# The stacks of the first two images, loaded one image at a time from two queues, at the seam between the two stages of a vision-transformer kernel

## The chip, the cores and the metric

The kernel runs on one core of a Trainium2 chip. The time is the device time of one execution in microseconds (us). The core has TensorE (PE in the profile, its weight loads PEld), VectorE (DVE), ScalarE (ACT), GpSimd (POOL) and the sync engine (SP). SP, ACT and POOL issue DMA transfers; the profile calls SP's and ACT's issuing SPq and ACTq. Each engine takes its instructions in order, so a wait or a transfer to be issued holds up all that is behind it on that engine. Sixteen DMA engines carry the transfers.

## The reference, cut to what matters

```python
h = concat([images] + four_shifted_crops).patches() @ W + b     # 128 images, 196 tokens, D = 192
h = concatenate([cls_tok, h], axis=1)                            # 197 tokens
xn = layernorm(h)
q, k, v = xn @ Wq.T, xn @ Wk.T, xn @ Wv.T                        # 6 heads of 32
scores = q @ k.T / sqrt(32) + lam * (q . anchor)                 # softmax over the keys
h = h + softmax(scores) @ v @ Wo.T
h = h + int8_quantised(layernorm(h) / 0.02) @ weight_t * 0.0002 + bias
```

## The kernel before

There are two stages. `build_tokens` makes the tokens of all 128 images, one row of patches at a time (14 rows), and writes the tokens and their normalised form to the DRAM scratches `h_dram` and `xn_dram`. `build_attention` then goes through the images with `images(eng, step)`: each engine runs `step(i)` for i = -5 to 131, and in one step different images are at different points of a pipeline. In step i, image i+5 is turned, image i+1 is scored, image i is exponentiated, image i-1 is attended, and older images go on through output projection and the last layer. Every engine has its own written order, with semaphores between them. Images 0 to 11 and the last 12 steps are written out; the middle is a loop over six images.

The work around the change, for one pair of images, is:

- `load_xn` (SP, L748 and L749) brings an image's normalised tokens to `xn_in`. PE turns them (`turn`, L822) into a PSUM bank, `MISC[2]`. ACT copies the rounded value to `x_hi` (L1052), DVE the rest to `x_lo` (L1219). PE waits for these before it turns the next image into the same bank (L1006).
- `project_block` (PE, L841) makes a block of q and k columns for both images of a pair at once: block 0 (q of heads 0 to 3), block 1 (q of heads 4 and 5, k of heads 0 and 1), block 2 (k of heads 2 to 5). ACT writes `qk_hi` (L1065) and DVE `qk_lo` (L1150). The partitions there are sorted by dimension and head. Before block 0 is written, ACT and DVE wait until the transfers of the pair before have landed (L1064, L1149), since these still read the buffer.
- `stack` (SP, L741) copies them within the on-chip memory to `q_st` and `k_st`, where each head has 32 partitions for each of three rows: q is stacked as high, high, low and k as high, low, high. That is 12 transfers for a pair: six of 128 packets of 1,584 bytes (198 values of one head for both images) and six of 64. All count on `stacked[pair]`, and `score(n, 0)` waits for 192 of it (12 times 16). Blocks 0 and 1 are made and stacked in an odd step, block 2 in the next, even one.
- `score` (PE, L873) multiplies q by k for one head, and DVE takes the maximum of each row (`maxima`, L1135). After six heads DVE splits the maxima (L1229, L1231), PE turns them (L1042), ACT copies them to `max_rows` (L1052), and SP puts them into two further partitions of `q_st` (L798). `score_t` (PE, L887) uses them, and `exps` (ACT, L1058) follows.

For pair 0, blocks 0 and 1 are made in step -3 and block 2 in step -2. Image 0 is scored in step -1, where also pair 2 (images 2 and 3) has its blocks 0 and 1. Image 1 is scored in step 0, image 2 in step 1, where image 0 is attended (L897).

Three things are done once between the stages. POOL fills the constant rows `key_rows` (L1315, L1317) and then works out the norm factors of the last tokens (L140 to L148). From the factors DVE makes the last `xn_t` (L1257), SP stores it (L804), and SP's first `load_xn` waits for it. ACT copies `key_rows` into all of `k_st` (L1125). POOL fills the maxima's rows of `q_st` (L1330).

Of the kernel before, what the change touches and what calls it, by code (L numbers as in the profile page):

```python
# [5 lines left out]
F32 = mybir.dt.float32  # L6
# [620 lines left out]
def build_attention(nc, s):  # L627
# [65 lines left out]
    stacked = [sem(f"stacked{i}") for i in range(NP)]  # L693
    max_landed = [sem(f"max_landed{i}") for i in range(MOD)]
# [41 lines left out]

    with nc.Block() as block:
        @block.sync
        def _(sp):
# [11 lines left out]
            def step(i):  # L751
# [6 lines left out]
                if p.within(B) and i.r % 2:  # L758
                    q_first, q_last, k_first = (0, 4), (4, H), (0, SPLIT)
                    q_rows, k_rows = slice(0, SPLIT * HD), slice(SPLIT * HD, BLOCK)  # L760
# [32 lines left out]
                if a.within(B):  # L793

                    if a.fixed and a.n == 0:
                        sp.wait_ge(no_score_made, 1)
                    sp.wait_ge(mrow_done, a.count(1, 1))
                    sp.dma_start(q_st[ST:ST + 2, a.pair, :, a.two, :].bitcast(F32), max_rows[:, a.two, :].bitcast(F32))\  # L798
                        .then_inc(max_landed[a.slot], 16)

# [16 lines left out]
        def _(pe):  # L817
# [48 lines left out]
            def score(n, h):  # L866

                if h == 0:
                    pe.wait_ge(stacked[n.pair], n.landed(192))
# [59 lines left out]
            def step(i):  # L929
# [70 lines left out]
                if has_f:  # L1000
# [4 lines left out]
                    elif f.plus(-1).within(B):  # L1005
                        pe.wait_ge(xhi_done, f.count(1, 0))  # L1006
                        pe.wait_ge(xlo_done, f.count(1, 0))
                    turn(MISC[2], xn_in, f.slot % NX, (DA, 2 * DB)).then_inc(xt_done, 1)
# [41 lines left out]
        def _(act):  # L1050
# [9 lines left out]
            def high(p, block, bank):  # L1060
                act.wait_ge(qk_done, p.pair_count(3, block + 1))
                if block == 0 and p.reuses(2):
                    before = p.plus(-2)
                    act.wait_ge(stacked[before.pair], before.landed(192))  # L1064
                nc.scalar.activation(qk_hi[:, block, :], bank[:, 0:2 * TP], ACT.Copy).then_inc(qkhi_done, 1)  # L1065

            def step(i):
# [10 lines left out]
                elif has_p:  # L1078
                    high(p, 2, MISC[2])
                    if has_c:  # L1080
                        exps(c, 5)
                if has_c:
# [7 lines left out]
                if has_f:  # L1090
# [3 lines left out]
                    copy(x_hi[:, f.pair, f.two, :, :], wide(MISC[2], DA), xhi_done)  # L1094
# [10 lines left out]
                if has_a:  # L1105
# [4 lines left out]
                    copy(max_rows[:, a.two, :], o_bank[0:2 * H, 1, 0:TP], mrow_done)  # L1110
                if has_g:
# [18 lines left out]
        def _(dve):  # L1130
# [14 lines left out]
            def low(p, block, bank):  # L1145
                dve.wait_ge(qkhi_done, p.pair_count(3, block + 1))
                if block == 0 and p.reuses(2):
                    before = p.plus(-2)
                    dve.wait_ge(stacked[before.pair], before.landed(192))  # L1149
                nc.vector.tensor_tensor(qk_lo[:, block, :], bank[:, 0:2 * TP], qk_hi[:, block, :].bitcast(F32),  # L1150
                                        ALU.subtract).then_inc(qklo_done, 1)

            def step(i):
# [60 lines left out]
                if has_f:  # L1214
# [3 lines left out]
                    for ic, rows_in in enumerate((DA, DB)):  # L1218
                        last = nc.vector.tensor_tensor(x_lo[0:rows_in, f.pair, f.two, ic, :],  # L1219
                                                       wide(MISC[2], rows_in)[:, ic, :],  # L1220
# [93 lines left out]

# [58 lines left out]
```

## Time and profile before

| | |
|---|---|
| time, median of 3 runs | 1737.6 us (1737.4 to 1737.8) |
| the profiled execution's own time | 1740.1 us |
| its span, first to last instruction | 1738.4 us |
| PE busy | 1649.2 us (95%) |
| DVE busy | 1471.8 us (85%) |
| POOL busy | 924.5 us (53%) |
| ACT busy | 759.3 us (44%) |
| last token work of the first stage to image 0's attention | 415 to 476 us |

Times of rows are us from the span's start. The clock of PE is given as a share of 2.4 GHz: 1.00 or 0.50 (1.2 GHz). A row of the timeline has its start, its duration, the engine, the line of the kernel, what it writes and reads, and in brackets how long the engine was idle before it and what ended that. The profiled execution's own time is 1.7 us over its span, and 2.5 us over the median of the runs.

### The profile page before, as it was taken

The numbers are of one execution on the slowest core, as the hardware profiler recorded it, in microseconds if no ns is written. First come the engines' busy times: TensorE is split into PE (matmuls) and PEld (weight loads), VectorE is DVE, ScalarE is ACT, GpSimd is POOL, SyncE is SP. The second block draws the span as 40 slices with busy tenths as digits, with TensorE's granted clock in tenths as the row PEclk, the third lists the DMA queues.
The fourth block names the chain that finished last, engine by engine and source line by source line (L and its number), as shares of the span: only waits on it lengthen the run. The fifth ranks groups of instructions, "written<-read, shape, count | busy, mean of one in ns | idle before, by whom it ended". The sixth has DMA issues, their size and how long they took to land.

```text
span 1738.4 us, 53263 instructions
## 1 busy us (share of the span) xinstructions
PE 1649.2 (95%) x16368; PEld 1500.8 (86%) x16368; DVE 1471.8 (85%) x3906; ACT 759.3 (44%) x1751; POOL 924.5 (53%) x1911
## 2 busy tenths in 40 slices
PE   4999999996599999999999999999999999999996
PEld 4999999995588888888888888888888888888884
DVE  7888888895388888888888888888888888888885
ACT  2000000001255555655556565555656555565653
POOL 3353443536056555555655565565556555555555
PEclk9999999997699999999999999999999999999998
DMA  9899989973787778877788777878787777877761
GB/s 300 269 306 298 322 283 307 325 250 131 114 141 154 143 137 149 147 150 144 139 147 150 146 142 146 147 148 150 134 150 150 146 143 142 147 148 148 139 122 33
DMA packets 214814, 303.66 MB, mean 175 GB/s; under 512 B 47584, under 2 KB 203667, under 8 KB 204644
## 3 DMA queue, kind: packets, MB, share of 16 engines
q1 hardware_dynamic: 204718, 228.10, 65.4%
q10 hardware_dynamic: 6054, 38.54, 7.5%
q0 software_dynamic: 3984, 36.28, 5.4%
q8 instruction: 32, 0.52, 0.1%
q14 instruction: 26, 0.21, 0.0%
HBM read 126.54 MB, written 58.29 MB: 106 GB/s over the span
## 4 chain that ended last, share of the span: by engine, by line
PE 46%; DVE 8%; POOL 8%; issue 7%; DMA 3%; SPq 2%; ACT 0%; POOLq 0%; DVEq 0%; ACTq 0%
PE bank L841 8%; PE o_bank L897 7%; PE bank L887 6%; PE bank L873 6%; PE bank L850 4%; PE bank L862 4%; PE o_bank L822 2%; POOL ln L163 2%; DMA k_st<-qk_lo 2%; DVE neg_max L1135 2%; POOL qx L1309 2%; PE o_bank L925 2%; PE o_bank L916 2%; PE bank L822 2%; PE bank L972 2%
## 5 line engine op out<-in xcount | busy, mean ns | idle before, releaser
L1058 ACT ACTIVATE probs<-bank 99x396 f32<-99x396 f32 x768 | 381.8, 497 | 218.8 <-PE bank L887 218.5
L1276 POOL TENSOR_TENSOR key_sum<-probs 99x396 f32<-99x396 f32 x256 | 227.5, 889 | 438.5 <-ACT probs L1058 289.6
L1135 DVE TENSOR_REDUCE neg_max<-bank 99x2 f32<-99x394 f32 x768 | 419.7, 561 | 25.7 <-PE bank L873 21.8
L340 PE MATMUL bank<-e_t,xt 128*128 128x192 f32 x2352 | 388.0, 329 | 25.4 <-DVE xt L448 21.7
L340 PEld LDWEIGHTS bank<-e_t,xt 128*128 128x128 f32 x2352 | 386.4, 192 | 26.6 <-DVE xt L448 26.4
L873 PE MATMUL bank<-k_st,q_st 96*99 96x198 f32 x1536 | 275.0, 274 | 17.8 <-DMA k_st<-qk_lo 11.6
L887 PE MATMUL bank<-q_st,k_st 99*99 99x198 f32 x1536 | 280.9, 264 | 6.9 <-DMA q_st<-max_rows 4.1
L448 DVE STREAM_TRANSPOSE xt<-x_t 128x256 f32<-128x256 f32 x588 | 215.0, 416 | 45.0 <-PE bank L340 43.5
L887 PEld LDWEIGHTS bank<-q_st,k_st 99*99 99x99 f32 x1536 | 207.9, 166 | 51.7 <-issue 44.3
L873 PEld LDWEIGHTS bank<-k_st,q_st 96*99 96x99 f32 x1536 | 192.7, 167 | 34.4 <-issue 13.5
L897 PE MATMUL o_bank<-probs,vals 99*32 99x198 f32 (+1 forms) x3072 | 197.1, 335 | 0.0
L1052 ACT ACTIVATE o_t<-o_bank 128x396 f32<-128x396 f32 x128 | 64.1, 501 | 232.6 <-PE o_bank L916 232.6
L897 PEld LDWEIGHTS o_bank<-probs,vals 99*32 99x32 f32 (+1 forms) x3072 | 112.9, 109 | 46.3 <-ACT probs L1058 0.2
L916 PE MATMUL o_bank<-key_sum,pick 99*32 99x198 f32 x1536 | 150.8, 330 | 0.0
L1309 POOL TENSOR_SCALAR qx<-h,ln 99x192 f32<-99x192 f32 x256 | 127.0, 503 | 40.1 <-POOL ln L163 40.1
L1288 POOL TENSOR_TENSOR hb<-h,ffn_bias 99x384 f32<-99x384 f32 x128 | 129.2, 1009 | 2.7 <-DVE h L1197 2.7
L349 ACT ACTIVATE ffn_w_bf<-ffn_raw 96x384 bf16<-96x384 int8 x1 | 0.5, 522 | 294.4 <-issue 294.4
L163 POOL TENSOR_TENSOR ln<-ln,minus_half 99x2 f32<-99x2 f32 x128 | 114.1, 892 | 23.1 <-POOL ln L162 23.1
L1150 DVE TENSOR_TENSOR qk_lo<-bank,qk_hi 128x396 fp32r<-128x396 f32 x192 | 108.3, 564 | 18.8 <-ACT qk_hi L1065 17.7
L1065 ACT ACTIVATE qk_hi<-bank 128x396 fp32r<-128x396 f32 x192 | 96.1, 501 | 60.4 <-PE bank L841 54.0
L862 PE MATMUL bank<-wo_hi,a_mix 128*99 128x192 f32 x512 | 120.3, 253 | 0.0
L862 PE MATMUL bank<-wo_lo,a_mix 128*99 128x192 f32 x512 | 120.2, 253 | 0.0
(134 smaller groups left out, 3589.4 us busy)
## 6 DMA issues: line engine op xcount, KB each, us to landing
x_t<-in_x_dram SPq DMA_DIRECT2D x26, 1344.0 KB, 20.5
x_t<-in_x_dram ACTq DMA_DIRECT2D x26, 1344.0 KB, 22.0
q_st<-qk_hi SPq DMA_DIRECT2D x128, 198.0 KB, 4.3
k_st<-qk_hi SPq DMA_DIRECT2D x128, 198.0 KB, 4.5
xn_in<-xn_scratch SPq DMA_DIRECT2D x128, 148.5 KB
h_in<-h_scratch SPq DMA_DIRECT2D x128, 148.5 KB
h_scratch<-h_t POOLq DMA_DIRECT2D x13, 1344.0 KB, 17.7
xn_scratch<-xn_t POOLq DMA_DIRECT2D x13, 1344.0 KB, 8.0
```

Source lines behind the costliest of these rows:

```text
L163: link(nc.gpsimd.tensor_tensor(v[6], v[5], half, ALU.pow))
L340: last = pe.matmul(token_bank(p)[:, 0:D], xt[:, p, c // 3, c % 3, :], e_t[:, row_kind(t), col, c // 3, c % 3, :], start=c == 0, stop=c == 5)
L448: last = nc.vector.transpose(xt[:, p, :, c, :].rearrange("p m (g b) -> p g m b", b=32), pix[:, c])
L862: last = pe.matmul(bank[0:TC, c * D:(c + 1) * D], inputs, weights, start=i == 0, stop=i == len(pairs) - 1)
L873: last = pe.matmul(S_BANK[h % 2][0:TC, c * TP:(c + 1) * TP], q_st[0:ST, n.pair, h, n.two, c * TC:(c + 1) * TC], k_st[0:ST, n.pair, h, n.tw ...
L887: last = pe.matmul(T_BANK[0:TC, c * TP:(c + 1) * TP], k_st[:, n.pair, h, n.two, c * TC:(c + 1) * TC], q_st[:, n.pair, h, n.two, :], start= ...
L897: pe.matmul(o_bank[at % 4 * HD:(at % 4 + 1) * HD, 0, col:col + TP], vals[0:kk, n.two, kc, h, :], probs[0:kk, n.two, h, kc, :], start=kc == ...
L916: last = pe.matmul(o_bank[to:to + HD, 0, TP:2 * TP], pick[:, j, :], key_sum[:, n.two, HEAD_AT[side * HG + j], :], start=j == 0, stop=j == ...
L1058: nc.scalar.activation(probs[:, n.two, h, :, :], wide(T_BANK, TC), ACT.Exp).then_inc(exp_done, 1)
L1135: nc.vector.tensor_reduce(out=neg_max[:, n.two, :, h], in_=wide(S_BANK[h % 2], TC)[:, :, 0:NTOK], axis=AX_X, op=ALU.max, negate=True).then ...
L1276: nc.gpsimd.tensor_tensor(key_sum[:, b.two, heads, :], probs[:, b.two, heads, 0, :], probs[:, b.two, heads, 1, :], ALU.add).then_inc(pool_ ...
L1309: nc.gpsimd.tensor_scalar(qx[:, e.two, cc, :], h1[:, e.two, cc, :], v[7][:, cc:cc + 1], v[6][:, cc:cc + 1], ALU.add, ALU.mult).then_inc(ln ...
```

## The change

For images 0 and 1 alone, the transfers of the stack take one image each (24 transfers of 792-byte packets in place of 12 of 1,584). SP issues those of q and ACT those of k, image 0's first. Image 0 counts on a semaphore of its own. The maxima's rows of images 0 and 1 are stored by ACT and no longer by SP. Image 1 is turned into `MISC[0]` in place of `MISC[2]`, without the wait for image 0's copies. POOL works out the last norm factors before it fills `key_rows`. The code for all later images is as it was.

```diff
+    first_stacked = sem("first_stacked")
...
+    def leads(n):
+        return n.fixed and 0 <= n.n < 2
+    def stack_one(eng, image, dst, row, heads, src):
+        eng.dma_start(dst[row * HD:(row + 1) * HD, 0, heads[0]:heads[1], image, :].bitcast(F32),
+                      src[:, image * TP:(image + 1) * TP].bitcast(F32))\
+            .then_inc(stacked[0] if image else first_stacked, 16)
+    def store_max_rows(eng, a):
+        if a.fixed and a.n == 0:
+            eng.wait_ge(no_score_made, 1)
+        eng.wait_ge(mrow_done, a.count(1, 1))
+        eng.dma_start(q_st[ST:ST + 2, a.pair, :, a.two, :].bitcast(F32), max_rows[:, a.two, :].bitcast(F32))\
+            .then_inc(max_landed[a.slot], 16)
+    def turned_into(f):
+        return MISC[0] if f.fixed and f.n == 1 else MISC[2]
...
+                if leads(p) and i.r % 2:
+                    sp.wait_ge(qkhi_done, p.pair_count(3, 1))
+                    stack_one(sp, 0, q_st, 0, q_first, qk_hi[:, 0, :])
+                    stack_one(sp, 0, q_st, 1, q_first, qk_hi[:, 0, :])
+                    sp.wait_ge(qklo_done, p.pair_count(3, 1))
+                    stack_one(sp, 0, q_st, 2, q_first, qk_lo[:, 0, :])
+                    sp.wait_ge(qkhi_done, p.pair_count(3, 2))
+                    stack_one(sp, 0, q_st, 0, q_last, qk_hi[q_rows, 1, :])
+                    stack_one(sp, 0, q_st, 1, q_last, qk_hi[q_rows, 1, :])
+                    sp.wait_ge(qklo_done, p.pair_count(3, 2))
+                    stack_one(sp, 0, q_st, 2, q_last, qk_lo[q_rows, 1, :])
+                elif leads(p):
+                    stack_one(sp, 1, q_st, 0, q_first, qk_hi[:, 0, :])
+                    stack_one(sp, 1, q_st, 1, q_first, qk_hi[:, 0, :])
+                    stack_one(sp, 1, q_st, 2, q_first, qk_lo[:, 0, :])
+                    stack_one(sp, 1, q_st, 0, q_last, qk_hi[q_rows, 1, :])
+                    stack_one(sp, 1, q_st, 1, q_last, qk_hi[q_rows, 1, :])
+                    stack_one(sp, 1, q_st, 2, q_last, qk_lo[q_rows, 1, :])
+                elif p.within(B) and i.r % 2:
...
-                if a.within(B):
-                    if a.fixed and a.n == 0:
-                        sp.wait_ge(no_score_made, 1)
-                    sp.wait_ge(mrow_done, a.count(1, 1))
-                    sp.dma_start(q_st[ST:ST + 2, a.pair, :, a.two, :].bitcast(F32), max_rows[:, a.two, :].bitcast(F32))\
-                        .then_inc(max_landed[a.slot], 16)
+                if a.within(B) and not leads(a):
+                    store_max_rows(sp, a)
...
-                if h == 0:
+                if h == 0 and n.fixed and n.n == 0:
+                    pe.wait_ge(first_stacked, 192)
+                elif h == 0:
                     pe.wait_ge(stacked[n.pair], n.landed(192))
...
-                    elif f.plus(-1).within(B):
+                    elif f.plus(-1).within(B) and not leads(f):
                         pe.wait_ge(xhi_done, f.count(1, 0))
                         pe.wait_ge(xlo_done, f.count(1, 0))
-                    turn(MISC[2], xn_in, f.slot % NX, (DA, 2 * DB)).then_inc(xt_done, 1)
+                    turn(turned_into(f), xn_in, f.slot % NX, (DA, 2 * DB)).then_inc(xt_done, 1)
...
                     act.wait_ge(stacked[before.pair], before.landed(192))
+                    if leads(before):
+                        act.wait_ge(first_stacked, 192)
...
+                k_rows, k_first, k_last = slice(SPLIT * HD, BLOCK), (0, SPLIT), (SPLIT, H)
+                if leads(p) and odd:
+                    act.wait_ge(qkhi_done, p.pair_count(3, 2))
+                    stack_one(act, 0, k_st, 0, k_first, qk_hi[k_rows, 1, :])
+                    stack_one(act, 0, k_st, 2, k_first, qk_hi[k_rows, 1, :])
+                    act.wait_ge(qklo_done, p.pair_count(3, 2))
+                    stack_one(act, 0, k_st, 1, k_first, qk_lo[k_rows, 1, :])
+                elif leads(p):
+                    act.wait_ge(qkhi_done, p.pair_count(3, 3))
+                    stack_one(act, 0, k_st, 0, k_last, qk_hi[:, 2, :])
+                    stack_one(act, 0, k_st, 2, k_last, qk_hi[:, 2, :])
+                    act.wait_ge(qklo_done, p.pair_count(3, 3))
+                    stack_one(act, 0, k_st, 1, k_last, qk_lo[:, 2, :])
+                    stack_one(act, 1, k_st, 0, k_first, qk_hi[k_rows, 1, :])
+                    stack_one(act, 1, k_st, 2, k_first, qk_hi[k_rows, 1, :])
+                    stack_one(act, 1, k_st, 1, k_first, qk_lo[k_rows, 1, :])
+                    stack_one(act, 1, k_st, 0, k_last, qk_hi[:, 2, :])
+                    stack_one(act, 1, k_st, 2, k_last, qk_hi[:, 2, :])
+                    stack_one(act, 1, k_st, 1, k_last, qk_lo[:, 2, :])
...
-                    copy(x_hi[:, f.pair, f.two, :, :], wide(MISC[2], DA), xhi_done)
+                    copy(x_hi[:, f.pair, f.two, :, :], wide(turned_into(f), DA), xhi_done)
...
                     copy(max_rows[:, a.two, :], o_bank[0:2 * H, 1, 0:TP], mrow_done)
+                    if leads(a):
+                        store_max_rows(act, a)
...
+            made = [0]
+            def link_last(ins):
+                made[0] += 1
+                ins.then_inc(last_row_ln, 1)
+                pool.wait_ge(last_row_ln, made[0])
+            norm_factors(nc, link_last, stats[:, LAST, EARLY:G, :], [ln[:, LAST, i, EARLY:G] for i in range(8)],
+                         minus_half[:, 0:G - EARLY])
 
             pool.memset(key_rows[ST:ST + 3, :], 1.0).then_inc(rows_made, 1)
             pool.wait_ge(rows_made, 1)
...
-            made = [0]
-            def link_last(ins):
-                made[0] += 1
-                ins.then_inc(last_row_ln, 1)
-                pool.wait_ge(last_row_ln, made[0])
-            norm_factors(nc, link_last, stats[:, LAST, EARLY:G, :], [ln[:, LAST, i, EARLY:G] for i in range(8)],
-                         minus_half[:, 0:G - EARLY])
             pool.wait_ge(last_row_xn, G - EARLY)
```

DVE's wait at L1149 and its read of the bank at L1220 are changed as ACT's are.

## Rows read from the trace of the kernel before

**Rows 1.** The chain of work that ended last, 380 to 495 us: start, us, what.
```profile
415.41 0.27 POOL key_rows L1315
...
416.18 0.22 POOL ln L140
...
421.71 2.78 DMA xn_scratch<-xn_t
...
434.37 0.73 SPq L741
...
443.23 7.99 DMA k_st<-qk_lo
...
461.36 3.27 DMA q_st<-max_rows
...
491.38 0.61 PE bank L873 x4
...
494.22 0.96 PE o_bank L897 x18
```

**Rows 2.** Timeline of the loads and projections, 416 to 442 us.
```profile
416.13 6.14 ACT L1052 ACTIVATE k_st<-key_rows 3x7128 fp32r<-3x7128 f32 x1 [84.43 <-POOL key_rows L1317]
...
425.74 0.40 SPq L749 DMA_DIRECT2D xn_in<-xn_scratch  x1
...
427.35 0.89 PE L822 MATMUL bank<-ident,xn_in 99*128 99x99 f32 x4 [14.04 <-DMA xn_in<-xn_scratch]
...
429.58 0.89 PE L822 MATMUL bank<-ident,xn_in 99*128 99x99 f32 x4 [1.34 <-DVE x_lo L1219]
...
435.49 0.50 ACT L1065 ACTIVATE qk_hi<-bank 128x396 fp32r<-128x396 f32 x1 [1.15 <-PE bank L841]
...
436.15 0.50 ACT L1052 ACTIVATE x_hi<-bank 128x396 fp32r<-128x396 f32 x1 [0.16 <-PE bank L822]
...
439.48 0.50 ACT L1065 ACTIVATE qk_hi<-bank 128x396 fp32r<-128x396 f32 x1 [2.83 <-PE bank L841]
```

**Rows 3.** Issue times of lines 261 and 741 (ns: least/median/most); landing of the latter.
```profile
L261 SPq DMA_DIRECT2D x_t<-in_x_dram x16: 433/482/2285, 3.7 to 15.4; - x16
L261 ACTq DMA_DIRECT2D x_t<-in_x_dram x16: 351/500/804, 6.6 to 14.8; - x16
...
L741 SPq DMA_DIRECT2D k_st<-qk_hi x256: 567/598/1966, 438.1 to 1681.0; - x128
...
DMA to landing us min/median/max: 2.8/4.6/8.0
```

**Rows 4.** DMA queue in 438 to 440, 443 to 445, 425 to 430: packets, MB, share.
```profile
q1 hardware_dynamic: 186, 0.26, 106.4%
...
q1 hardware_dynamic: 359, 0.30, 115.1%
...
q1 hardware_dynamic: 1429, 0.74, 57.0%
```

**Rows 5.** Timeline of images 0 to 2, 451 to 476 us.
```profile
453.98 0.50 ACT L1065 ACTIVATE qk_hi<-bank 128x396 fp32r<-128x396 f32 x1 [11.82 <-PE bank L841]
...
459.22 0.33 ACT L1052 ACTIVATE max_rows<-o_bank 12x198 fp32r<-12x198 f32 x1 [2.82 <-PE o_bank L1042]
...
464.37 0.61 SPq L741 DMA_DIRECT2D k_st<-qk_lo  x1
...
471.23 0.96 PE L873 MATMUL bank<-k_st,q_st 96*99 96x198 f32 x4
...
475.67 1.04 PE L897 MATMUL o_bank<-probs,vals 99*32 99x198 f32 x18
```

**Rows 6.** Busy time of PE, PEld, DVE, ACT, POOL by stretch, clock, DMA share, GB/s.
```profile
457.90:461.30 3.40, 2.19 (x18) 1.82 (x16) 2.12 (x7) 1.20 (x3) 0.00 (x0) 1.00 1.08 143
461.30:464.70 3.40, 0.00 (x0) 0.00 (x0) 0.79 (x2) 0.00 (x0) 0.00 (x0) 1.00 0.97 175
464.70:468.10 3.40, 3.08 (x16) 2.80 (x16) 1.01 (x2) 1.61 (x4) 0.85 (x1) 0.50 1.09 134
```

More of the change, by code:

```diff
@@ L757, in step @@
                     load_xn(ahead)
-                if p.within(B) and i.r % 2:
-                    q_first, q_last, k_first = (0, 4), (4, H), (0, SPLIT)
-                    q_rows, k_rows = slice(0, SPLIT * HD), slice(SPLIT * HD, BLOCK)
+                q_first, q_last, k_first = (0, 4), (4, H), (0, SPLIT)
+                q_rows, k_rows = slice(0, SPLIT * HD), slice(SPLIT * HD, BLOCK)
+                if leads(p) and i.r % 2:
[17 more added lines that the diff above has]
+                elif p.within(B) and i.r % 2:
                     sp.wait_ge(qkhi_done, p.pair_count(3, 1))
@@ L1149, in low @@
                     dve.wait_ge(stacked[before.pair], before.landed(192))
+                    if leads(before):
+                        dve.wait_ge(first_stacked, 192)
                 nc.vector.tensor_tensor(qk_lo[:, block, :], bank[:, 0:2 * TP], qk_hi[:, block, :].bitcast(F32),
@@ L1219, in step @@
                         last = nc.vector.tensor_tensor(x_lo[0:rows_in, f.pair, f.two, ic, :],
-                                                       wide(MISC[2], rows_in)[:, ic, :],
+                                                       wide(turned_into(f), rows_in)[:, ic, :],
                                                        x_hi[0:rows_in, f.pair, f.two, ic, :].bitcast(F32), ALU.subtract)
@@ L1310, in step @@
                                             v[6][:, cc:cc + 1], ALU.add, ALU.mult).then_inc(ln2_step, 1)
-            pool.memset(key_rows[ST:ST + 3, :], 1.0).then_inc(rows_made, 1)
-            pool.wait_ge(rows_made, 1)
-            pool.affine_select(out=key_rows[ST:ST + 3, 0:NTOK], in_=key_rows[ST:ST + 3, 0:NTOK], compare_op=ALU.is_ge,
-                               fill=0.0, base=1, pattern=[[0, NTOK]], channel_multiplier=-1).then_inc(rows_made, 1)
-            pool.wait_ge(rows_made, 2)
             made = [0]
@@ L1328, in _ @@
                          minus_half[:, 0:G - EARLY])
+            pool.memset(key_rows[ST:ST + 3, :], 1.0).then_inc(rows_made, 1)
+            pool.wait_ge(rows_made, 1)
+            pool.affine_select(out=key_rows[ST:ST + 3, 0:NTOK], in_=key_rows[ST:ST + 3, 0:NTOK], compare_op=ALU.is_ge,
+                               fill=0.0, base=1, pattern=[[0, NTOK]], channel_multiplier=-1).then_inc(rows_made, 1)
+            pool.wait_ge(rows_made, 2)
             pool.wait_ge(last_row_xn, G - EARLY)
```

## The prediction

> **What bounds the kernel now.** I read the chain of work that ended last first, around the change of stage. It goes through each thing that the diff touches: POOL's constant rows, the norm factors, the store and load of the last tokens, two turns, the projections, a series of issues of SP, and then the last transfer of the first stack, which is 7.99 us under way. PE starts on image 0's scores at 451.22. Ten microseconds later the chain waits again, for the maxima's rows, issued at 461.36 and landed at 464.63 [rows 1]. The timeline gives the starts between these [rows 2, 5], the stretches the clock [rows 6], the lines' own view what an issue costs [rows 3], and the DMA view what a packet costs [rows 4]. All of this is start-up, and it happens once. From image 2 on the code is the same, and what comes later waits for PE, DVE and POOL through semaphores and for no fixed moment, so what the start-up gains or loses should stay to the end. The whole question is by how much image 0's attention, now at 475.67 [rows 5], moves.
>
> **Step 1, the constant rows.** The norm factors start at 415.41 in place of 416.18 [rows 1]: 0.77 us less on the path. What moves behind them is ACT's copy of 6.14 us, which began at 416.13 [rows 2]. The nine factor instructions end near 419.1, POOL's two instructions 0.7 later, so the copy runs from 419.8 to 426.0. ACT is wanted for image 0 when the first turn ends, 427.35 + 0.89 - 0.77 = 427.5 [rows 2]. It is covered with 1.5 us to spare. If POOL must wait behind DVE's work on the last tokens until 420.9, 0.4 us comes back.
>
> **Step 2, the other bank.** Image 1's turn starts at 429.58, 1.34 after the first ends, having waited for the copies of image 0 [rows 2]. In another bank that wait goes: at most 1.34. But its tokens are issued up to 425.74 + 0.40, one load behind image 0's. I take 1.0 (bounds 0 and 1.34). The first stack transfer goes out at 434.37 - 0.77 - 1.0 = 432.6 [rows 1].
>
> **Step 3, what ACT's transfers hold up.** ACT's issues cost what SP's do (0.50 to 0.48 where both load), and a stack's costs 0.60 [rows 3]. ACT sends three right after `qk_hi` of block 1, now at 435.49 + 0.50 - 1.77 = 434.2. Behind them in ACT's order is `x_hi` of image 2, on which block 2 waits by way of `x_lo`. It would start at 436.15 - 1.77 = 434.4 [rows 2], and starts after 3 x 0.64 at 436.15. So block 2 gains nothing: its `qk_hi` is written at 439.5 as before. The last transfer of image 0's k goes out at 439.5 + 0.5 + 2 x 0.64 = 441.3, against 443.23, since it is the third and not the twelfth in its queue. Six more for image 1 end at 445.8. Only then comes `x_hi` of image 3, done in `x_lo` by 447.0, which pair 2's block 0 needs.
>
> **Step 4, image 0's stack lands.** 441.3 plus 2.8 to 7.99 [rows 1, 3]. The longest was with 11 others ahead. Here image 1's q is in the way. I take 4.7: 446.0 (444.1 to 449.3), five microseconds earlier than before.
>
> **Step 5, image 1's stack is the next wait.** PE can score heads 0 and 1 of image 0 and make pair 2's block 0, which takes 2.7 (451.26 to 453.98) and so ends at 448.8 or, by `x_lo`, 449. But the copies out of it wait for both semaphores, that is for image 1's transfers too, because `qk_hi` and `qk_lo` are read until then. On DVE `qk_lo` stands ahead of the maxima of heads 2 to 5, so image 0 waits as well. When does image 1 land? Before, 1152 packets of 1,584 bytes and the loads between them took from 434.37 to 451.22, 16.85 us, with the DMA engines full. Now there are 2304 packets of 792. A packet cost 2 us x 16 x 1.064 / 186 = 183 ns at a mean of 1.4 KB, and 2 x 16 x 1.151 / 359 = 103 ns at 0.84 KB; with nothing behind them loads' packets of 0.52 KB cost 5 x 16 x 0.57 / 1429 = 32 ns [rows 4]. So cost goes nearly by bytes: half the size is 0.55 of the price. 1152 x 183 ns / 16 is 13.2 us of packets, and the new ones take 1.1 times as long, 1.3 more. 432.6 + 16.85 + 1.3 = 450.8; I take 451.0. The bounds are 449.5 (nothing added) and, with 183 ns for every packet however short, 432.6 + 16.85 + 13.2 = 462.6.
>
> **Step 6, the maxima's rows.** From pair 2's first `qk_hi` to `max_rows` is 459.22 - 453.98 = 5.24, then 0.33 for it [rows 5]. ACT issues at once, where SP had nine stack transfers to send first, until 461.36. The transfer takes 3.27 in that crowd [rows 1], perhaps 2.3 without one; I take 3.0. `score_t` of image 0 starts at 451.0 + 0.1 + 5.24 + 0.33 + 3.0 + 0.1 = 459.8, against 464.8: 5.0 us gained.
>
> **Step 7, pair 2's stack and the clock.** SP sends k's last part of pair 2 after its own nine. Before, at 464.37, with the maxima's issue (0.7) between; now at 464.37 - 2.9 - 0.7 = 460.8, as it starts at 451.6 and not 454.5. It lands some 5.8 later, 466.6, and image 2's first scores, before at 471.23, wait for it: 4.6 gained. Before, TensorE stood from 460.7 to 464.8 (0.00 busy in 461.3 to 464.7), and the granted clock went from 1.00 to 0.50 (2.4 to 1.2 GHz); with 2.19 of 3.40 busy it had stayed [rows 6]. Now the holes are about 2 and 3 us, no stretch is empty, and I take the clock to stay. From those scores to the attention it took 475.67 - 471.23 = 4.44 at the low clock [rows 5], but 494.22 - 491.38 = 2.84 a pair later at the high one [rows 1]: 1.6 more. **Sum: 4.6 + 1.6 = 6.2 us.** The profiled execution would take 1740.1 - 6.2 = 1733.9. It lies 2.5 over the median of the runs, so the median becomes 1731.4.
>
> The Trainium skill ("DMA: Bandwidth & Descriptors", Rules for kernel authors) says that spreading transfers over SP, ACT and GpSimd gives no bandwidth, since all run on the same 16 DMA engines, and saves issue time alone. By it step 5 would have no faster end at all. No row of this trace has two full queues side by side.
>
> **The rivals.** What 0.2% is here, 3.5 us, is about what a measurement can tell from no change.
>
> - Likeliest, 54%: the above. Its own range is step 5 at 449.5 to 452.5 and step 7 with 1 us either way: 4.3 to 8, so 1729.6 to 1733.3.
> - Faster still, 10%: the two queues write different partitions at once and image 1 lands by 448, so that PE alone sets block 0's copies at 448.8. The gain is 5.2 + 2.2 (step 6) + 1.0 of clock: 1729.2. For it: at a share of 1.08 the engines moved 143 GB/s and at 0.97 175 GB/s [rows 6], so it is not the number of engines alone that sets the rate. Against: the share is full already with one queue, 1.06 to 1.15 [rows 4]. The Trainium skill ("SBUF — State Buffer", Door 1: The DMA port swizzle) puts partitions 0 to 63 on one half of the ports and 64 to 127 on the other, which is what could let q and k rows pass each other.
> - Partly lost, 16%: a short packet costs 0.65 of a long one (image 1 lands at 453.5) and TensorE's clock falls as before. 464.8 - 462.3 = 2.5 gained, none from the clock: 1735.1.
> - It doesn't do what it says, 8%: image 0 starts earlier, but pair 2's block 0, its stack and the maxima's rows all end as late as ever for ACT's nine issues and the wait for image 1, and only steps 1 and 2 remain: 1.8 gained, 1735.8.
> - Slower, 12%: cost goes by packets. The most is 462.6 in step 5, 8.6 after 453.98; less 2.1 for step 6 it is 6.5 lost, 1744.1. It turns to a loss where image 1 lands after 456, that is where a 792-byte packet costs over 0.75 of one of 1,584 (137 ns). The 103 ns speak against it, but those packets came from DRAM, and no row has on-chip packets of 792 bytes in a crowd.
>
> **How the numbers follow.** The likeliest gives 1731.4. Down to 1728.5 takes in nearly all of the faster case; up to 1738.5 takes in both cases of little gain and the near half of the slower one. Faster by over 0.2% is the first two, 0.64; within it, the next two, 0.24; slower 0.12.
>
> **What would show it.** Steps 1 and 2: the last tokens' store issued 0.8 earlier, a second turn right behind the first, the first stack issue near 432.6. Step 3: ACT's `x_hi` of image 2 still at 436. Steps 4 and 5: image 0's scores near 446, and pair 2's first `qk_hi` waiting for a transfer until 451; the number to look at. Step 6: `score_t` near 459.8. Step 7: clock 1.00 from 455 on, attention at 469.5. The prediction is wrong if packets of half the size cost well over half, if ACT's issues take far over 0.6 with full queues, or if the clock falls again.

## The result, and the profile after

The changed kernel takes 1735.98 us (median of 15 runs, 1732.44 to 1738.53), the kernel before, run beside it, 1738.18 (15 runs, 1737.0 to 1743.06). The ratio is 0.9983, with an interval of 0.9976 to 0.9991: some 2.9 us or 0.17% faster (the medians lie 2.2 us apart). The forecast was a gain of 6.2 us. The time lies inside the range (1728.5 to 1738.5), above the likeliest case's own 1729.6 to 1733.3, and by the 0.2% bound it counts as no change, to which I had given 0.24. That it lies inside is owed to the width of the range, which took in the cases of little gain; the gain is under half of what the sum gave.

The chain of work of the changed kernel that ended last, from 420 to 490 us (start, us, what), against [rows 1]:

```profile
421.98 2.77 DMA xn_scratch<-xn_t
...
426.01 2.92 DMA xn_in<-xn_scratch
428.98 0.94 PE bank L855 x4
...
431.24 3.65 PE bank L874 x10
...
435.45 0.69 ACTq L744
...
441.34 0.58 ACTq L744
...
446.53 1.84 DMA k_st<-qk_lo
448.51 2.00 PE bank L874 x5
450.53 0.51 ACT qk_hi L1102
451.06 0.57 SPq L762
...
460.24 7.48 DMA k_st<-qk_lo
467.76 0.98 PE bank L908 x4
...
489.10 0.62 PE bank L908 x4
```

The wait for image 0's stack is gone from it. In its place stand ScalarE's own issues, three at 435.45 and nine from 441.34. Then comes pair 2's stack, whose last transfer is 7.48 us under way. The start of image 4's scores, the last row, moved from 491.38 [rows 1] to 489.10, the 2.3 us of the whole.

The timeline of the same kernel shows the starts that answer to [rows 2, 5]:

```profile
428.98 0.92 PE L855 MATMUL bank<-ident,xn_in 99*128 99x99 f32 x4 [0.41 <-DMA xn_in<-xn_scratch]
...
437.48 0.50 ACT L1087 ACTIVATE x_hi<-bank 128x396 fp32r<-128x396 f32 x1 [2.06 <-issue]
...
445.97 0.98 PE L908 MATMUL bank<-k_st,q_st 96*99 96x198 f32 x4 [3.02 <-DMA k_st<-qk_lo]
...
447.20 0.50 ACT L1087 ACTIVATE x_hi<-bank 128x396 fp32r<-128x396 f32 x1 [5.89 <-issue]
...
456.36 0.33 ACT L1087 ACTIVATE max_rows<-o_bank 12x198 fp32r<-12x198 f32 x1 [2.35 <-PE o_bank L1077]
...
460.72 0.62 PE L922 MATMUL bank<-q_st,k_st 99*99 99x198 f32 x2 [2.92 <-DMA q_st<-max_rows]
...
467.76 0.98 PE L908 MATMUL bank<-k_st,q_st 96*99 96x198 f32 x4 [0.28 <-DMA k_st<-qk_lo]
...
472.74 1.61 PE L932 MATMUL o_bank<-probs,vals 99*32 99x198 f32 x18
```

Where stage one ends differs from one profiled execution to the next by up to 4 us, in code that no kernel here changes. So I count every start from SP's store of the last tokens, `h_scratch<-h_t`, which was issued at 415.41 before and 416.29 after. By it, in us (the forecast is the prediction's moment less 415.41):

| start of | before | forecast | after | gained |
|---|---|---|---|---|
| first stack transfer | 18.96 | 17.2 | 17.51 | 1.45 |
| image 0's first scores | 35.85 | 30.6 | 29.68 | 6.17 |
| pair 2's first `qk_hi` | 38.57 | 35.7 | 34.24 | 4.33 |
| `max_rows` of image 0 | 43.81 | 40.9 | 40.07 | 3.74 |
| transposed scores of image 0 | 49.36 | 44.4 | 44.43 | 4.93 |
| image 2's first scores | 55.82 | 51.2 | 51.47 | 4.35 |
| attention of image 0 | 60.26 | 54.1 | 56.45 | 3.81 |

Of 3.81 us at attention, 0.58 goes behind it and 0.88 is stage one's difference in this pair of executions. 2.35 us are left between the spans, 1738.4 and 1736.1. The 0.58 is gone by the end of attention itself: from its first matmul to the copy of its result (`o_t`) it took 475.67 to 477.60, 1.93 us at a granted clock of 1.00, before, and 472.74 to 475.24, 2.50 us at a mean clock of 0.76, after.

### The profile page after: what moved, and what is told of

Read it like the earlier page. It is cut to its first block, busy times and chain, and to the rows that moved or that the text cites. A ratio compares the mean times of both kernels' runs of the same rounds, so it can differ in the third digit from the quotient of the medians.

```text
span 1736.1 us, 53274 instructions
## 1 busy us (share of the span) xinstructions
PE 1655.0 (95%) x16368; PEld 1504.7 (87%) x16368; DVE 1471.9 (85%) x3906; ACT 759.4 (44%) x1751; POOL 925.9 (53%) x1911
## 4 chain that ended last, share of the span: by engine, by line
PE 50%; DVE 8%; POOL 7%; issue 7%; DMA 2%; SPq 1%; ACT 0%; ACTq 0%; POOLq 0%; DVEq 0%
PE bank L874 9%; PE o_bank L932 8%; PE bank L922 6%; PE bank L908 6%; PE bank L895 5%; PE bank L883 5%; PE o_bank L855 3%; PE o_bank L951 2%; PE bank L855 2%; PE o_bank L960 2%; POOL ln L163 2%; DVE neg_max L1193 2%; PE bank L1007 2%; DMA k_st<-qk_lo 2%; POOL qx L1369 2%
## 6 DMA issues: line engine op xcount, KB each, us to landing
h_scratch<-h_t POOLq DMA_DIRECT2D x13, 1344.0 KB, 17.2
```

## The experiments

Each ratio is against the kernel before on the same chip, where not said otherwise.

### What makes image 1 land early: short packets, not the second queue

**e5** keeps both queues and sends whole pairs, packets of 1,584 bytes in 12 transfers.

```diff
-eng.dma_start(dst[..., image, :], src[:, image * TP:(image + 1) * TP])
+if image == 0:
+    eng.dma_start(dst[row * HD:(row + 1) * HD, 0, heads[0]:heads[1], :, :], src)
```

All twelve count on `stacked[0]` again, so image 0's scores wait for both images.

> The changed kernel, but each of the 12 transfers of pair 0 takes both images again (packets of 1,584 bytes), q from SP and k from ACT as in the change. Theory A (the short packets are what made the transfers land in 2.6 to 3.1 us): here they take 4 to 8 us as in the kernel before, a packet costs 150 to 200 ns, and image 0's scores start at 449 to 451. Rival B (two queues are what made it fast): landing stays near 3 us, a packet near 70 ns, and the scores start at 446 or earlier; the time is that of the changed kernel or less, since ACT has six issues and not twelve.

Measured: 1739.25 us, ratio 1.0 (0.999 to 1.0009). The changed kernel has 0.9983 (0.9976 to 0.9991) from other runs, and the two intervals just touch. Image 0's scores come at 34.73 from the store and pair 2's first `qk_hi` at 37.45. The DMA view of its 431 to 448 us (queue, packets, MB, share of 16 engines), landings below:

```profile
q1 hardware_dynamic: 1490, 1.31, 52.9%
q10 hardware_dynamic: 672, 0.91, 38.6%
...
q_st<-qk_hi SPq DMA_DIRECT2D x2, 198.0 KB, 4.3
k_st<-qk_hi ACTq DMA_DIRECT2D x2, 198.0 KB, 6.9
```

The changed kernel, 434 to 448.5 us, moves the same 2.24 MB:

```profile
DMA packets 3525, 2.24 MB, mean 154 GB/s; under 512 B 824, under 2 KB 3524, under 8 KB 3524
...
q1 hardware_dynamic: 2180, 1.32, 36.8%
q10 hardware_dynamic: 1344, 0.91, 27.7%
...
q_st<-qk_hi SPq DMA_DIRECT2D x4, 99.0 KB, 2.8
k_st<-qk_hi ACTq DMA_DIRECT2D x4, 99.0 KB, 3.1
```

The two queues with long packets fill 91.5% of 17 us of 16 engines, 249 us of packets. The short ones take 64.5% of 14.5 us, 150 us, though there are 1,362 packets more. Two queues alone gave nothing. e5 takes away two things at once, the short packets and image 0's coming first. For image 0's scores no run separates them, since none sends image 0 first in long packets. Pair 2's first `qk_hi`, which waits for both images, is a measure of the packets without the order, and it too came earlier with the short ones, 34.24 against 37.45.

**e3** is the kernel before with pair 0's 24 short transfers all on SP, image 0's first.

```diff
+if p.fixed and p.n in (0, 1):
+    one(0, dst, row, heads, src)          # image 0 now
+    later.append((dst, row, heads, src))  # image 1 behind all twelve
+    return
```

> The kernel before, but pair 0's stack goes image by image, all 24 transfers from SP's queue, image 0's twelve first. Theory A (short packets are cheap, one queue or two): each lands in 2.6 to 3.1 us, so image 0's scores start 2.8 us after the twelfth issue (443.8), at 446.7, 4.5 us earlier than in the kernel before. Rival B (two queues are needed): landing of 4 us and more, scores at 449 or later. Image 1's twelve issues last to 452 either way.

**e4** is the kernel before with each 198 KB transfer cut into two of 64 packets of 1,584 bytes.

```diff
+for j, landed in enumerate((stacked[0], half_stacked)):
+    at = row * HD + 16 * j
+    sp.dma_start(dst[at:at + 16, 0, heads[0]:heads[1], :, :],
+                 src[64 * j:64 * j + 64, :]).then_inc(landed, 16)
```

> The kernel before, but pair 0's six transfers of 128 packets are split in two of 64 packets of 1,584 bytes (16 rows each), 18 issues of 99 KB from SP. Theory A (the length of the packet is what costs): packets still take 150 to 200 ns in a crowd and land in 4 us and more. Rival B (the crowd is what costs: 198 KB per 0.6 us of issue is more than the engines move, and 99 KB per 0.6 us is not): packets of 1,584 bytes take about 70 ns, twice the 38 ns of the short ones, and land in about 3 us.

The DMA view of e3 in 437 to 439 us, then of e4 in 438 to 440 and in 442 to 444:

```profile
q1 hardware_dynamic: 432, 0.30, 47.2%
```

```profile
q1 hardware_dynamic: 193, 0.24, 48.6%
```

```profile
q1 hardware_dynamic: 256, 0.32, 100.4%
```

On one queue a short packet costs 2 x 16 x 0.472 / 432 = 35 ns, and the transfers land in 2.0 to 2.8 us. Image 0's scores stood at 30.16, 0.5 us behind the changed kernel. In e4 a packet cost 81 ns where the engines were half idle and 2 x 16 x 1.004 / 256 = 126 ns where they were full, and the scores came at 35.94, as before. So e4 bears out neither of its theories whole. Taken by themselves, pair 0's stack packets have these means in the traces: of 1,584 bytes 171 ns before, 172 in e5 and 132 in e4, of 792 bytes 43 in e3 and 49 in the changed kernel. e4 and the changed kernel hand over the same 1.8 MB in about the same time (12.9 and 13.3 us of issues), and pay 132 against 2 x 49 = 98 ns for 1,584 bytes: that is the length. The kernel before hands them over in 9.5 us and pays 171: that is the crowd. The length counts, with one queue or two, and so does how fast long packets follow each other. The second queue's use is another: in e3 SP has 24 issues, and pair 2's first `qk_hi` came at 37.97, where the changed kernel has 34.24. Each ran once (1743.61 and 1742.94, against a median of 1739.25 before), which says nothing of the time.

### What pair 2 waits for: ScalarE's issues

**e2** moves image 1's six k transfers behind ScalarE's copy `x_hi` of image 3.

```diff
 copy(x_hi[:, f.pair, f.two, :, :], wide(turned_into(f), DA), xhi_done)
+if leads(p) and not odd:
+    stack_one(act, 1, k_st, 0, k_first, qk_hi[k_rows, 1, :])
+    ... (the other five)
```

> The changed kernel, with ACT's six transfers of image 1's k behind its copy of image 3's x_hi instead of ahead of it. Theory A (ACT's nine issues, 5.9 us, are what pair 2's block 0 waits for, and image 1's landing is not): x_hi of image 3 comes at about 443.3 instead of 447.2, block 0 starts right behind the first two scores, at about 447.0 instead of 448.5, and its copy at 449.0, unless image 1 has not landed by then; 1.0 to 1.5 us less from the seam to image 0's score_t, and the time 1 to 1.5 us under the changed kernel's. Rival B (image 1's landing is the wait): its transfers now go out 0.5 later, so the copy comes at 451 or later and nothing is gained.

Measured: 1733.29 us, ratio 0.9962 (0.9949 to 0.9976). Its chain, 440 to 475 us:

```profile
443.01 0.50 ACT x_hi L1087
...
446.25 3.32 DMA k_st<-qk_lo
...
449.65 0.51 ACT qk_hi L1102
```

`x_hi` of image 3 comes at 27.12 from the store in place of 30.91, and the copy out of pair 2's block 0 now waits for image 1's last transfer, 446.25 + 3.32 = 449.57, as the prediction had wanted it. The copy of the maxima comes 1.45 us earlier (38.62).

**e13** repeats the same kernel beside e12 (below).

> ScalarE's order alone (the second image's six k transfers behind the copy of image 3's x_hi), a second time, so that it stands beside the last kernel on one chip with the same runs of the kernel before, and in more runs than the five of its first trial (0.9962 [0.9949, 0.9976]; the changed kernel 0.9983). If the order is worth what the first profile showed (1.45 us to the copy of the maxima, of which 0.4 was left at attention of image 0), the ratio is 0.996 to 0.998; if the first trial was chance, 0.998 or above, level with the changed kernel.

Measured: 1734.75 us, ratio 0.9965 (0.9952 to 0.9977), `max_rows` at 38.35. The order is worth what the first trial gave, by the ratios 3 to 4 us more than the changed kernel, which ran at another time (the two intervals together leave about 2.6 us either way). The traces show less: image 2's first scores came 0.4 (e2) and 0.7 us (e13) earlier than in the changed kernel, attention of image 0 0.4 and 1.3, the end 0.8 and 2.7, all from the store. What the gap between traces and times is was not tested. One profile is one execution, and even between before and after the lead moves: 3.8 us at attention, 4.9 halfway through the exponentials (1095.28 and 1091.27 of the traces), 3.2 at the end.

### Steps 1 and 2 by themselves

**e6** is the kernel before with the constants moved and the other bank.

```diff
+norm_factors(nc, link_last, ...)
 pool.memset(key_rows[ST:ST + 3, :], 1.0)
-elif f.plus(-1).within(B):
+elif f.plus(-1).within(B) and not (f.fixed and f.n < 2):
-    turn(MISC[2], xn_in, ...)
+    turn(turned_into(f), xn_in, ...)
```

> The kernel before with two parts of the change alone: the constants behind the norm factors, and image 1's turned tokens in another bank. The transfers and the row of maxima stay as before. Prediction's steps 1 and 2: the first issue of the stack stands 1.8 us earlier against the store of the last tokens (18.96 before, so 17.2; the changed kernel showed 17.51), and the time is 0.8 to 1.8 us below before. Rival: image 0's stack is set by bytes and packets, so that only half of the 1.45 us is left at the first scores (35.85 before), and the clock, which falls at 416.9 before, takes the rest: within 0.2% of before, 0 to 1 us.

Measured: 1739.0 us, ratio 0.9996 (0.9987 to 1.0005). The first issue came at 17.73, 1.23 us earlier, image 0's scores and pair 2's stack 1.18 earlier, attention of image 0 2.4 (57.82), since image 2's scores to attention took 3.67 us in place of 4.44. The times give 0.7 us (-0.9 to 2.3), which can't be told from nothing.

### Who stores the maxima's rows

**e7** is the changed kernel, with SP storing them. **e11** is the same on top of ScalarE's order.

```diff
-if a.within(B) and not leads(a):
+if a.within(B):
     store_max_rows(sp, a)
-if leads(a):
-    store_max_rows(act, a)
```

> The changed kernel, but SP stores the maxima's rows of the first two images, as before the change; everything else stays. Prediction's step 6: SP issues that row behind pair 2's first transfers, so the transposed scores of image 0 come up to 2 us later against the copy of the maxima than in the changed kernel (44.43 - 40.07 = 4.36 us there, 49.36 - 43.81 = 5.55 us before), 5.4 to 6.4 us, and the time is 1 to 2 us above the changed kernel's 1736.0. Rival (the path from the row is held by pair 2's k stack, whose last transfer landed at 467.7 in the changed kernel, so the row has slack): the transposed scores are later by the same amount, but attention and the time are within 0.5 us of the changed kernel's.

> The changed kernel with ScalarE's order (the second image's six k transfers behind the copy of image 3's x_hi) and the maxima's rows of the first two images stored by SP as before the change. SP storing that row cost nothing in the last trial (0.9975 against the changed kernel's 0.9983 of before), so if each edit stands alone this is level with the order alone, ratio 0.9955 to 0.997 of before. Rival (ScalarE's 0.76 us of issue delayed its exponentials): lower, 0.994 to 0.9955.

Measured: e7 1735.02 us, ratio 0.9975 (0.9964 to 0.9985), e11 1733.44, ratio 0.9966 (0.9951 to 0.998). Each is level with its kernel that has ScalarE store them. In e7 the transposed scores came 0.87 us later (45.30) and image 2's first scores 0.3 later (51.78), but attention of image 0 earlier (55.64 against 56.45), since the clock came back ahead of it (table below). The part of the change with the clearest gain on paper shows none here.

### TensorE's clock

**e8** fills TensorE's waits with dummy matmuls, the first 52 behind the wait for the constants. **e9** has 62 ahead of that wait and 8, 10 and 14 in three later holes. **e10** has the 62 alone. All three have ScalarE's order.

```diff
+def fill(count):
+    columns = wa_hi[:].rearrange("p w n -> p (w n)")
+    for _ in range(count):
+        pe.matmul(o_bank[0:BLOCK, 0, 0:2 * TP], columns[:, 0:BLOCK], columns[:, 0:2 * TP], start=True, stop=True)
+fill(62)
 pe.wait_ge(consts, 6)
```

> The changed kernel with ScalarE's order of the last experiment (the second image's six k transfers behind the copy of image 3's x_hi), and dummy matmuls that nobody reads, put where TensorE otherwise waits: 52 at the start of stage two, 8 ahead of the first scores of image 0, 14 ahead of the first transposed scores of image 0. Theory A (what the hole of 2.9 us at 457.8 to 460.7 and the long wait before 434 cost behind them is the clock): the granted clock is 2.4 GHz through the seam, a block of the projections (3.65 us in the changed kernel) takes about 1.9 us, the 5.8 us of TensorE's work between 460.7 and 467.0 take about 3, and attention of image 0 starts 3 us or more earlier against the store of the last tokens than the 56.05 of the last experiment; the time falls by 1.5 to 4 us below its 1733.3. Rival B (the clock stands beside the path, since transfers and ScalarE's issues set the seam's steps): the clock is high, but attention of image 0 starts within 1 us of 56.05 and the time is 1732 to 1735. Rival C (the dummy matmuls themselves delay the real ones): slower than 1733.3 by up to 2 us, with a wait for them in front of the turns at 427 to 429.

> The changed kernel with ScalarE's order of the earlier experiment (the second image's six k transfers behind the copy of image 3's x_hi), and dummy matmuls that nobody reads, this time ahead of TensorE's wait for the constants: 62 where stage one ends (at 414, so until 425 to 426 of the 427.2 at which the turns come), 8 ahead of pair 0's third block (hole of 3.25 us), 10 ahead of the first scores (3.28 us) and 14 ahead of the first transposed scores (3.49 us). The last trial put its first 52 behind the constants, from 424.05 to 436.3, 8.7 us past the turns' 427.67; behind that delay its seam was 2.4 us shorter (59.51 - 23.48 = 36.03 us from the first issue of the stack to attention of image 0, against 56.05 - 17.63 = 38.42). Theory A (the clock is on the path): the clock stays at 2.4 GHz to 440 at least, the first issue comes 0.5 to 1.5 us earlier than 17.63, attention of image 0 at 52.5 to 54.5 against the store of the last tokens, and the time is 1 to 3 us below the 1733.3 of ScalarE's order alone. Rival B (the seam hangs on transfers and issues, not on TensorE's pace): clock high and attention of image 0 at 55.5 or later, time 1732.5 to 1735.

> As the kernel beside it, with the 62 dummy matmuls where stage one ends alone, none in the later holes. Theory A: the first stretch of low clock begins some 10 us later than 418.8; pair 0's projections are short (3.65 to about 1.9 us a block of two), which brings half to two thirds of the gain of the kernel with all four places, since the clock falls again in the holes of 3 us at 438 and 446: 0.5 to 2 us below 1733.3. Rival B: no gain, 1732.5 to 1735.

Measured: e8 1742.11 us, ratio 1.0015 (1.0006 to 1.0024), since its first dummies ended at 436.5 and the turns waited for them. e9 1736.82, ratio 0.999 (0.998 to 0.9999). e10 1737.08, ratio 0.9987 (0.9978 to 0.9996). Stretches of e9 (us, busy time and count of PE, PEld, DVE, ACT, POOL, clock, DMA share, GB/s):

```profile
416.50:428.00 11.50, 11.50 (x62) 11.23 (x62) 3.30 (x12) 6.20 (x1) 9.30 (x12) 1.00 0.50 191
428.00:433.00 5.00, 1.92 (x13) 1.54 (x13) 1.25 (x4) 1.00 (x2) 0.35 (x1) 1.00 0.59 154
433.00:436.40 3.40, 3.40 (x14) 3.25 (x13) 1.14 (x2) 1.00 (x2) 0.00 (x0) 0.50 0.20 60
436.40:446.60 10.20, 5.39 (x31) 4.46 (x31) 2.00 (x7) 1.51 (x3) 0.00 (x0) 1.00 0.81 167
460.30:463.70 3.40, 2.16 (x16) 1.66 (x16) 1.25 (x3) 1.58 (x4) 0.62 (x1) 1.00 1.18 135
463.70:473.90 10.20, 8.81 (x46) 7.87 (x50) 4.09 (x11) 3.41 (x8) 1.16 (x2) 0.50 0.49 82
```

The clock stood at 2.4 GHz to 446.6, where the kernels without dummies have 1.2, but for one stretch: in 433.0 to 436.4, where TensorE was busy throughout with pair 0's blocks 0 and 1, it was at 1.2 here too. Image 0's scores came at 29.52, against 30.07 and 30.01 in the two runs of the order alone, and attention at 56.61, no earlier. From the second turn (13.90 after the store, 12.83 in e13) to the scores, 1.6 us were gained, and 1.1 had been lost ahead of it: the store of the last tokens took 3.42 us to land and their load 3.45 (2.77 and 2.92 in the changed kernel). In e10 the store took 3.92; in the twelve other profiles, none with dummies beside it, it took 2.8. The load tells nothing, as e11, without dummies, has 3.56. Why the store lands later beside the dummies was not tested. So the higher clock gave back some 1.6 us ahead of image 0's scores, with blocks 0 and 1 left low; what it would give there too no run shows. As a whole the dummies brought no gain, rather a loss of some 4 us against the order alone (e11, on the same chip, has 0.9966). Little of that loss stands at attention of image 0 (55.97 in e10, 56.05 and 55.17 in e2 and e13). From there to the end e9 took 1265.4 us and e10 1264.0, against 1262.9 and 1261.9 in e2 and e13, and the cause of that is open.

### Pair 2's stack

**e12** is the kernel with ScalarE's order, with SP made to wait for the copy of the maxima where it stored them before, so that its next loads come no earlier.

```diff
-if a.within(B) and not leads(a):
-    store_max_rows(sp, a)
+if leads(a):
+    sp.wait_ge(mrow_done, a.count(1, 1))
+elif a.within(B):
+    store_max_rows(sp, a)
```

> The changed kernel with ScalarE's order (the second image's six k transfers behind the copy of image 3's x_hi); ScalarE still stores the maxima's rows of the first two images, but SP waits for each of those copies at the place where it stored the row before, so that its loads of the next image's tokens come no earlier than in the kernel before. In the changed kernel those loads (148.5 and 49.5 KB) were issued 3.0 us behind the last transfer of pair 2's stack, and image 2's first scores waited for it (issued at 43.95, read at 51.47 against the store of the last tokens); in the kernels where SP stored the row the loads came 8 us behind it and no such wait stood in the profile. Theory A (the loads that SP sends early fall on pair 2's stack): no wait for that stack, the scores at most 6.9 us behind the last issue, attention of image 0 within 10.5 us of its first transposed scores (12.0 and 12.5 in the two kernels with early loads), so at 54 to 54.5, and the time 0.5 to 2 us below that of the order alone, run beside it. Rival B (pair 2's stack takes 7.5 us whatever follows it): the wait stays, time level. Rival C (the wait goes, but what it held up ends elsewhere, at the next pair's transfers or the clock): profile as in A, time within 0.5 us of the order alone.

Measured: 1735.93 us, ratio 0.9973 (0.9964 to 0.9982), not faster than e13 beside it. The loads went out at 50.17, 7.1 us behind the stack's last issue, and the wait stayed. PE's waits of e12, 450 to 474 us (us in total, times, longest):

```profile
PE bank L924 <- DMA q_st<-max_rows: 3.5, 1, 3.5
PE bank L910 <- DMA k_st<-qk_lo: 0.9, 1, 0.9
```

So theory A fell and rival B held: the later loads have no part in it. What does set it can be read by laying the kernels side by side. From the first issue of pair 2's stack to image 2's first scores it takes

| kernel | first issue to scores, us | scores to attention, us | mean clock from scores to attention |
|---|---|---|---|
| before | 16.72 | 4.44 | 0.58 |
| after | 16.70 | 4.98 | 0.50 |
| e2, e13 | 16.77, 16.74 | 4.99, 4.42 | 0.50, 0.58 |
| e12 | 16.74 | 4.47 | 0.58 |
| e5 | 16.73 | 4.92 | 0.51 |
| e7, e11 | 16.74, 16.69 | 3.86, 3.72 | 0.68, 0.72 |
| e3, e4, e6 | 16.68, 16.33, 16.23 | 3.79, 3.62, 3.67 | 0.70, 0.74, 0.73 |
| e8, e9, e10 | 17.06, 17.10, 17.44 | 3.58, 4.98, 3.55 | 0.76, 0.50, 0.76 |

In after, e2, e13, e12, e5 and e9 the trace marks the scores as waiting for `k_st<-qk_lo`, the stack's last transfer: 16.70 to 16.77 us behind the first issue in five of them, 17.10 in e9, whether the last issue comes 9.1 us behind the first (e12) or more, and whatever follows on the queue. In the others no wait is marked: TensorE gets there by way of the maxima's rows and the transposed scores, and needs about as long (16.69 and 16.74 in e11 and e7), so the stack has landed by then, in e6 within 16.23. The two ways are level: the marked waits are 0.3 (after) to 1.0 us long, and to shorten the second alone, as ScalarE's store of the maxima does, leaves the first. In the changed kernel the queue is 93% busy over that time, 451 to 467.7 us:

```profile
q1 hardware_dynamic: 2147, 2.22, 93.0%
```

That is 0.930 x 16.7 x 16 = 248 us of packets, as many as pair 0's stack took before (0.921 x 17 x 16 = 250, 434.3 to 451.3). So in the kernels with the mark the 1,584-byte packets of pair 2 set when image 2 can start, and of what was tried here only an earlier first issue moved it. This is a reading of the traces; no run gave pair 2 short packets.

## Why the prediction was right or wrong

The moments below are from the store, as in the table of the result, where no other time is named.

- **Step 1** held in mechanism: the norm factors start 0.02 us behind the store, 0.75 earlier, and the copy of 6.14 us ended at 426.9 of the trace, covered. Only 0.56 us of it was left at the first turn. The six instructions that make `xn_t` took 1.99 us in place of 1.84.
- **Step 2** held: the two turns start 1.31 us apart in place of 2.23, 0.92 gained against the 1.0 taken. The second waits 0.41 us for its tokens, since its load is one behind image 0's, as that step allowed. The two steps gave 1.45 in place of 1.77 (1.23 in e6).
- **Step 3** held in mechanism and nearly in size: an issue costs ScalarE 0.62 us, and `x_hi` of image 2 did not come earlier (21.19, before 20.74). The last six issues ended at 30.86, forecast 30.4.
- **Step 4** held in mechanism: scores at 29.68, forecast 30.6. Image 0's last k transfer was issued at 26.33, 0.4 later than forecast, and landed 3.3 us behind its issue, not 4.7.
- **Step 5** failed. It said that half the size costs 0.55 of the price, so that twice as many packets take 1.1 times as long. They took 114 us in all in place of 197, which is 49 ns each against 171, or 0.29 of the price. Image 1 had landed by 32.08, not at 35.6. What held pair 2's `qk_hi` was step 3's own nine issues, by way of `x_hi` of image 3 at 30.91. It came at 34.24, 1.5 earlier than forecast and not 3.5. e2 and e13 show the cause: with the issues behind the copy, `x_hi` comes 3.8 us earlier and the copy out of block 0 waits for the transfer. How much that is worth at the end is less clear (0.8 and 2.7 us in the traces, some 3 in the times).
- **Step 6** came out for the transposed scores (44.43, forecast 44.4) by two errors that cancel. They started from a `qk_hi` 1.5 earlier, but from it to `max_rows` it took 5.83 us and not 5.24, and the row landed some 3.9 us behind its issue and not 3.0. Nor does the gain lead on, as e7 and e11 show: attention stands behind image 2's scores, and these behind pair 2's stack as well as the maxima.
- **Step 7** failed in its clock term, and its first term came out (4.35 against 4.6) by luck. The stack lands 7.48 us behind its last issue, not 5.8, but that issue came at 43.95, 1.4 earlier than forecast, for step 5's error. The last transfer stands behind the whole stack in a queue that is 93% busy from the first issue on. [rows 1] had shown it for pair 0: 434.37 to 451.22, 16.85 us. Pair 2's first issue at 34.77 and 16.7 us give the measured 51.47. Before, no wait for that stack is marked ahead of the 471.23, so not all of it was its landing, as the step took for granted. And the clock term of +1.6 became -0.5. The step took it that holes of 2 and 3 us leave the clock high. TensorE stood still for 2.90 us, from 457.80 to 460.70 of the trace, and the clock fell:

```profile
457.80:460.70 2.90, 0.00 (x1) 0.01 (x1) 1.05 (x2) 0.66 (x2) 0.00 (x0) 0.93 1.05 173
460.70:464.10 3.40, 3.13 (x16) 2.79 (x16) 1.06 (x3) 1.66 (x4) 0.89 (x1) 0.50 1.14 123
464.10:467.50 3.40, 3.12 (x17) 2.58 (x16) 1.43 (x6) 1.15 (x3) 0.88 (x1) 0.50 0.77 118
467.50:473.90 6.40, 6.14 (x34) 5.47 (x38) 3.13 (x6) 2.28 (x6) 0.00 (x0) 0.50 0.31 60
```

It stayed low from image 2's first scores to the start of image 0's attention, 4.98 us at a mean clock of 0.50. Before, that took 4.44 at a mean of 0.58, since the clock came back at the end of it. The table above holds the spread: 3.6 to 3.9 us at means of 0.68 to 0.76, 4.4 to 4.5 at 0.58, 4.9 to 5.0 at 0.50 or 0.51. No run kept the clock high from image 0's transposed scores on (in e9 it fell at 463.7 all the same), so the price of this term is read from the traces and was not tested.

So the sum of 6.2 reads 4.35 - 0.54 = 3.81 us in the profile, less 0.6 in attention itself, and the times give 2.9 (1.6 to 4.2). Nearly all of what is missing at attention, 2.14 of 2.39 us, is the clock term. Of the rivals, "faster still" had its condition met: image 1 landed by 32.08 (its 448 is 32.6 from the store), and block 0, not the transfer, set the copies. But that was not for its reason, the two queues (e5), and its gain of 8.4 did not follow. In time "partly lost" (1735.1) and "doesn't do what it says" (1735.8) lie nearest. The second named ScalarE's nine issues, the right cause, but its size was wrong: pair 2 gained 4.3 us, not 1.8. "Slower", by the number of packets, was refuted: a packet of half the size costs less than half. The Trainium skill's rule that spreading over queues gives no bandwidth ("DMA: Bandwidth & Descriptors", Rules for kernel authors) agrees with e5, ratio 1.0, and it saves issue time alone, as e3 against the changed kernel shows. The path by which step 5 used it, no faster end at all, did not follow, since the packet's size had changed too.

What stays open: why e9's and e10's last tokens were stored more slowly and where the rest of their loss comes from, why the times of e2 and e13 gain more than their traces show at the seam, what the clock term would be worth with the hole closed, and what pair 2's stack in short packets would give. The fastest kernel here is e2 (e13), with e11 level, 0.35 to 0.38% ahead of before, and by the ratios about 0.2% ahead of the changed kernel, whose runs were not beside it.

## What to carry to other kernels

Where a batch of transfers keeps the queue busy from its first issue on, cost it from there, by its whole traffic (here 16.7 to 17.1 us where it was the wait), and not from the last issue plus a median landing. Before a compute engine is given DMA issues, lay its next copy beside them: here nine issues of 0.62 us stood in front of one copy, and with six of them moved behind it the copy came 3.8 us earlier. Where a sum counts on a high clock, look at the holes in front of the stretch. And when a price is drawn from two rows that differ in source as well as in size, keep it wide on both sides; here the bound below was missing.

## What the runs showed of the hardware

- On-chip packets of 792 bytes, each to its own row of the stack, cost 43 ns (e3, one queue) and 49 ns (changed kernel, two queues) as a mean over pair 0's stack, 35 in e3's emptier stretch. Those of 1,584 bytes cost 171 ns before, 172 in e5 and 132 in e4, where they are handed over more slowly, and there 81 with half idle engines and 126 with full ones. With the loads among them, the same 2.2 MB take 150 us of packet time in place of 250. The landing of a transfer falls from 4.3 to 8.0 us to 2.2 to 3.6.
- The granted clock fell to 1.2 GHz behind 2.9 us without a matmul (457.80 to 460.70), and in e9 it fell at 463.7 too, where 14 dummies had filled the hole down to 0.88 us.
- The store of the last tokens (576 KB) landed in 2.8 us in twelve profiles, and in 3.4 and 3.9 us in the two (e9, e10) in which 62 dummy matmuls ran beside it.
